# Gated cross attention with routed experts: value stores, attention's first loads and the last y store under other waits

## The reference

```python
def _L0_xattn_ref(x, cross_input, ...):
    q, k, v = _heads(x @ Wq + bq), _heads(x @ Wk + bk), _heads(x @ Wv + bv)
    att = jnp.einsum('bhqd,bhkd->bhqk', q, k) * scale
    att = jnp.where(causal[None, None], att, -jnp.inf)
    y = jnp.einsum('bhqk,bhkd->bhqd', jax.nn.softmax(att, axis=-1), v)
    ...
    y = y + jnp.einsum('bhqk,bhkd->bhqd', jax.nn.softmax(attc, axis=-1), vc)
    return y @ Wp + bp

x = x + jnp.tanh(g_xattn[0]) * _L0_xattn_ref(_layernorm(x, axis=-1), ctx_512, ...)
x = x + jnp.tanh(g_ffn[0]) * _L0_ffn_ref(_layernorm(x, axis=-1), ...)
```

## Time and profile before

| | us |
|---|---|
| median of 3 runs | 2671.09 |
| lowest and highest | 2663.04, 2671.52 |
| the profiled execution | 2655.1 |
| its span | 2653.1 |

### The profile page before, as it was taken

One profiled execution on the slowest core, in us unless ns is written; L12 is line 12 of the kernel. 1 busy time (PEld: TensorE's weight loads), 2 busy tenths in 40 slices (PEclk: granted clock), 3 DMA queues, 4 the chain that ended last, 5 costly groups with the idle time before them and its releaser, 6 DMA issues. The chain is left out here.

```text
span 2653.1 us, 55050 instructions
## 1 busy us (share of the span) xinstructions
PE 2456.7 (93%) x20198; PEld 1487.9 (56%) x20198; DVE 1927.3 (73%) x3194; ACT 1574.4 (59%) x3344; POOL 462.5 (17%) x534
## 2 busy tenths in 40 slices
PE   6886999999999999999999999988999999998897
PEld 6775444444444444444444444477788877787785
DVE  8766888888888888888888888566533644544557
ACT  4441577777777777777777777843244433442442
POOL 2001100101010101010010101022332423422514
PEclk9897899999999999999999999987999999999998
DMA  7999674756566564747465654242134322422533
GB/s 255 395 363 289 90 106 77 96 84 85 91 79 89 80 96 65 104 65 95 81 89 87 82 86 69 55 154 98 57 121 127 116 70 78 120 68 68 170 102 104
DMA packets 163778, 305.66 MB, mean 115 GB/s; under 512 B 44455, under 2 KB 111150, under 8 KB 155182
## 3 DMA queue, kind: packets, MB, share of 16 engines
q1 hardware_dynamic: 150174, 265.53, 48.1%
q0 software_dynamic: 12288, 33.57, 4.0%
q10 hardware_dynamic: 1072, 3.23, 0.5%
HBM read 165.10 MB, written 127.68 MB: 110 GB/s over the span
## 5 line engine op out<-in xcount | busy, mean ns | idle before, releaser
L811 ACT ACTIVATE at_P<-at_ST 128x512 f32<-128x512 f32 (+4 forms) x2176 | 1095.9, 559 | 372.5 <-PE at_ST L854 350.3
L762 DVE TENSOR_REDUCE f_part<-at_R 128x2 f32<-128x804 f32 x1024 | 976.0, 994 | 121.4 <-PE at_R L842 117.0
L869 PE MATMUL at_OP<-at_P,at_V 128*32 128x256 f32 x8192 | 642.0, 385 | 16.0 <-ACT at_O L819 12.9
L854 PE MATMUL at_ST<-at_Q,at_K 64*128 64x512 f32 (+4 forms) x1428 | 343.7, 455 | 3.5 <-ACT at_P L811 3.5
L869 PEld LDWEIGHTS at_OP<-at_P,at_V 128*32 128x32 f32 x8192 | 163.3, 108 | 264.2 <-ACT at_P L811 185.7
L842 PE MATMUL at_R<-at_K,at_Q 64*128 64x402 f32 x1344 | 271.2, 392 | 5.1 <-DVE f_part L762 5.1
L745 POOL TENSOR_SCALAR_AFFINE_SELECT at_P<-at_P 128x512 f32<-128x512 f32 x128 | 81.6, 637 | 1089.1 <-ACT at_P L811 1089.1
L854 PEld LDWEIGHTS at_ST<-at_Q,at_K 64*128 64x128 f32 (+1 forms) x1428 | 141.6, 180 | 218.5 <-ACT at_P L811 203.6
L759 DVE TENSOR_REDUCE f_mx<-at_R 128x2 f32<-128x256 f32 (+3 forms) x256 | 209.9, 821 | 42.8 <-PE at_R L835 40.7
L1825 DVE TENSOR_TENSOR ex_ab<-ex_bank,ex_sg 128x256 f32<-128x256 f32 x148 | 62.8, 424 | 226.1 <-ACT ex_sg L1908 167.4
L842 PEld LDWEIGHTS at_R<-at_K,at_Q 64*128 64x128 f32 x1344 | 128.0, 185 | 115.8 <-issue 69.2
(11 more groups left out here) (246 smaller groups left out, 4170.3 us busy)
## 6 DMA issues: line engine op xcount, KB each, us to landing
at_K<-k_parts SPq DMA_DIRECT2D x126, 264.1 KB, 9.2
k_parts<-pj_kpart SPq DMA_DIRECT2D x32, 800.5 KB, 8.5
expert_rows<-ex_rb SPq DMA_DIRECT2D x148, 128.0 KB
ex_xb<-sorted SPq DMA_DIRECT2D x72, 256.0 KB
v_items<-pj_vbuf SPq DMA_DIRECT2D x32, 544.0 KB, 8.0
q_parts<-pj_qpart SPq DMA_DIRECT2D x32, 512.0 KB, 10.6
at_Q<-q_parts SPq DMA_DIRECT2D x252, 64.0 KB, 9.6
f_K<-k_parts SPq DMA_DIRECT2D x60, 264.1 KB, 9.9
```

Source lines behind the costliest of these rows:

```text
L762: dve.tensor_reduce(part[:, :, p, q, c], buf[:, :, 0:XC], AX.X, ALU.max).then_inc(s_drain, 1)
L811: act.activation(Pt[(NKT * n + s) % NP][0:rows, h, c0:T], ST[(NST * n + s * G + h) % NB][0:rows, c0:T], ACT.Exp, scale=SCALE).then_inc(s_e ...
L854: pe.matmul(ST[t % NB][0:rows, c0:T], K[n % NU][half, p, keys], Q[n % NU][half, kind, p, c0:T], start=True, stop=True).then_inc(s_st, 1)
L869: ins = pe.matmul(OP[32 * h:32 * h + 2 * D, at], V[n % 2][0:rows, key_tile(s), h, :], Pt[(NKT * n + s) % NP][0:rows, h, at], start=s in (0 ...
```

## The change

The four value stores of a batch become one that covers the same rows; the value tag's semaphore counts 16 a batch instead of 64. SP's `load(1)` waits for batch 0's stores only, and ahead of the first load of each later batch's items SP waits for that batch's stores. GpSimd fills `K1`'s ones first, and waits for the stores and fills `V`'s ones behind it; the thresholds of `s_one` follow this order. The last y store counts up a semaphore of its own, `s_ylast`; SP no longer waits for it at the end of attention, but in `load_y` of the last batch.

```diff
 def written(tag, batches):
-    return (64 if tag == "v" else 32) * batches + 1
+    return (16 if tag == "v" else 32) * batches + 1
...
-                    for g in range(NG):
-                        dst = VS.rearrange("(b g) p t c -> b g p t c", b=B)[bass.ds(b, 1), g]
-                        sp.dma_start(dst.rearrange("o p t c -> (o p) t c"), vbuf[:, g]).then_inc(s_wr["v"], 16)
+                    dst = VS.rearrange("(b g) p t c -> b p g (t c)", b=B)[bass.ds(b, 1)]
+                    sp.dma_start(dst.rearrange("o p g c -> (o p) g c"), vbuf[:, :, :, :].rearrange("p g t c -> p g (t c)")
+                                 ).then_inc(s_wr["v"], 16)
...
-                            dve.wait_ge(s_wr["v"], 64 * b + 1)
+                            dve.wait_ge(s_wr["v"], 16 * b + 1)
...
                         if r == 2 and n < NU:
-                            sp.wait_ge(s_one, 2 * n + 2)
+                            sp.wait_ge(s_one, 4 * (n - 1) + 2)
...
-                    sp.dma_start(YS[n // NG, :, :, n % NG * GC:(n % NG + 1) * GC], ysum[n % 2][:, :, :]).then_inc(s_yst[n % 2], 16)
-
-                for n in WRITES:
-                    sp.wait_ge(first.s_wr[n], written(n, B))
+                    sp.dma_start(YS[n // NG, :, :, n % NG * GC:(n % NG + 1) * GC], ysum[n % 2][:, :, :]).then_inc(
+                        s_yst[n % 2] if n < NI - 1 else early.s_ylast, 16)
+
+                def batch_written(b):
+                    for n in WRITES:
+                        sp.wait_ge(first.s_wr[n], written(n, b + 1))
+
+                batch_written(0)
                 load(1)
...
                     if n + 2 < NI:
+                        if (n + 2) % NG == 0:
+                            batch_written((n + 2) // NG)
                         load(n + 2)
...
                 for u in range(2):
-                    sp.wait_ge(s_yst[u], 16 * (NI // 2))
+                    sp.wait_ge(s_yst[u], 16 * ((NI - u) // 2))
...
                     if b >= 2:
                         sp.wait_ge(s_T, b - 1)
+                    if b == B - 1:
+                        sp.wait_ge(early.s_ylast, 16)
                     sp.dma_start(y[b % 2][:, :, :], YS[b]).then_inc(s_y[b % 2], 16)
```

More of the change, by code:

```diff
@@ L712, in _ @@
             def _(pool):
[L713 to L716, removed]
                 def ones(n):
                     for h in range(2):
-                        pool.wait_ge(s_one, 2 * n + h)
+                        if n > 1 or h:
+                            pool.wait_ge(s_one, 4 * (n - 1) + h)
                         pool.memset(K[n][64 * h + 32:64 * h + 64, :, :].bitcast(F32), 1.0).then_inc(s_one, 1)
-                    pool.wait_ge(s_one, 2 * n + 2)
+                    pool.wait_ge(s_one, 4 * (n - 1) + 2)
                 def values(n):
@@ L734, in _ @@
                 ones(1)
+                for n in WRITES:
+                    pool.wait_ge(first.s_wr[n], written(n, B))
+                for u in range(2):
+                    pool.memset(V[u][:, :, :, D:2 * D], 1.0).then_inc(s_one, 1)
                 values(0)
@@ L916, in __init__ @@
         self.s_y, self.s_w, self.s_b, self.s_r = (r_.sem(n) for n in ("y0", "w", "b", "r"))
+        self.s_ylast = r_.sem("ylast")
         self.s_f = [r_.sem(f"f{u}") for u in range(2)]
```

## The result

| | before | after |
|---|---|---|
| median | 2666.78 us (16 runs) | 2660.16 us (16 runs) |
| lowest and highest | 2660.92, 2674.18 | 2651.1, 2666.29 |
| the profiled execution's span | 2653.1 us | 2664.3 us |

The ratio is 0.9975, with a 95% interval of 0.9964 to 0.9986: 6.7 us less, between 3.7 and 9.6. The forecast was a ratio of 0.9981, 5.1 us. The interval holds it.

What follows compares the result with a forecast made beforehand. Transfers were taken to bound projection, and TensorE, ScalarE and VectorE together to pace attention. Terms 3.4 + 0 + 0 + 1.7 = 5.1 us gave ratio 0.9981, 2666.0 us from a median of 2671.09; range 2656 to 2676.

Steps and rivals of the forecast that it cites:

- The rounds: Projection's 8 rounds: one value store lands when four did, so VectorE's wait in 7 rounds stays; 0 us.
- C: Rival, projection rounds: the single store lands earlier, VectorE's wait shrinks 1.5 us each, 10.5 us more off; 2655.4, chance 0.12.
- D: Rival, projection rounds: the single store drains slower, VectorE's wait grows, 1.8 us a round; 2678.6, chance 0.10.
- The estimate beside C: Projection rounds: by the skill's fixed part, four stores 13.1 us, one 7.1; 6 us a round, 42 in all.
- The first border: Projection to attention: all engines wait for SP's four issues, 3.97 us; a single one takes 0.59, saving 3.4 us.
- B: Rival, first border: SP must stay for the whole single store, so only 1.7 us come off; 2669.4, chance 0.17.
- The loads: Start of attention: loads waiting for their own batch and ones filled at once move up, but nobody waits; 0 us.
- The second border: Attention to mixing: SP no longer awaits the last y store's landing; 1.7 us off on all engines.
- TensorE's clock (E): Rival, both borders: shorter gaps keep TensorE's clock high, 2.4 us more off; 2663.6, chance 0.17.
- The sum: Whole kernel: 3.4 us at the first border, 1.7 at the second, 0 elsewhere; 5.1 us, ratio 0.9981.

Runs made afterwards that it cites:

- e9: The kernel before with one value store per batch plus a second of the same bytes to a spare tensor, awaited too: 2641.60 us, ratio 1.0162.
- e6: The kernel before with one value store in batches 0 to 6 and four in the last: 2597.96 us, ratio 1.0002.
- e1: The kernel before with only the value stores made one per batch; loads, ones and last y store as before: 2596.42 us, ratio 0.9994.
- e5: The kernel before with one value store in the last batch alone, four in batches 0 to 6: 2596.85 us, ratio 0.9989.
- e3: The kernel before with only the loads waiting for their own batch and K1's ones filled first; four value stores: 2598.14 us, ratio 1.0001.
- e12: The changed kernel, but GpSimd waits for the stores and fills V's ones before K1's, as before: 2593.21 us, ratio 0.9977 against before.
- e4: The whole change on the second experiment chip, against the kernel before: 2591.31 us, ratio 0.9973.
- e2: The kernel before with only the last y store on its own semaphore, awaited by batch 7's load: 2595.86 us, ratio 0.9987.
- e11: The kernel before with one value store per batch and item 0's context shift rows issued by ScalarE on its queue: 2603.75 us, ratio 1.0024.

## Why the prediction was right, point by point

**The rounds, 0: right.** VectorE waits 43.9 us instead of 45.9, and between 41.4 and 46.2 in all traces but e9's. That bytes and not transfers set the rounds is shown by e6 and e9 together. C and D fall. The estimate beside C, 42 us by the Trainium skill's fixed part, rested on a fit for transfers that GpSimd issues, and nothing of it is seen.

**The first border, 3.4 us: right in place and nearly in size.** The issue takes 0.38 us and not the 0.59 taken from the y rows; from it to the first matmul 4.42 us became 0.83: 3.6. That SP might have to stay (B) falls. The nearest row was x's 0.38 with as many rows, not the y rows' 0.59.

**The loads, worth 0: this step failed.** The prediction said that "the load is 6 us early today" and that "what is moved up also costs nothing", and of the border that "all of it stands 3.4 us earlier". It looked for the readers of `K1` and found them late. It named item 0's shift rows, 16 KB in all, only as the next thing on SP's queue, and left out that they lie behind the load in the same line and that TensorE's first scores need them. load(1) starts at the landing of the stores, and the border's edit does not move that, while it moves the scores 3.6 us up. Without the loads' part TensorE waits 3.8 us (e1) or 2.5 us (e5), and the gain of 3.6 is gone or mostly gone. So the part is worth 0 alone (e3, ratio 1.0001) and, by the waits, up to 3.8 us behind the border's edit. The first half of the part, waiting for the own batch, brings this; of the early ones no effect is seen (e12). The sum came out right because the change holds both; that was luck, for nothing in the prediction says that the two parts need each other.

**The second border, 1.7 us: right in place, 1.5 in size.** With the landing no longer awaited, the first matmul comes 0.7 us after SP's issue ends, not the 0.5 us that it came after the landing.

**TensorE's clock (E): half seen, worth nothing.** Behind the gap of 1.8 us the clock stays high at first, but falls within the phase of maxima, as the argument against E said: the windows of after have 0.65 from 240 to 244 and 0.50 from 244 on, and it is still 0.50 at the first scores. The first exponential comes 38.08 us behind the first matmul in after and 38.33 in before, so 0.25 us at most came of it. At the second border the eight transposes take 1.94 us as before, behind a gap of 2.9.

**The sum.** The traces give 3.6 + 1.5 = 5.1 us, the forecast's own sum. The measured 6.7 us, and 7.0 by the ratio in e4 (7.7 by the medians), lie above it, and 5.1 lies within both intervals (3.7 to 9.6, 4.4 to 9.4). The nearest to a surplus is e2, 3.4 us where its trace shows 1.5, again within its interval. Whether 2 us more come off somewhere is open: of the stretches looked at, the rounds, the rest of attention and what follows show nothing beyond their spread of 4 to 5 us, which is wider than that.

## What to carry to other kernels

Before an issue or a wait is cut from a border, list what starts by another clock, here loads that wait for a landing, and what small transfer lies behind them in the line: the stage moves up, they do not, and the smallest copy may become the last. Price parts of a change in the company in which they will run, since two edits can be worth next to nothing alone and 3.4 us together. Where SP leads a border, count the issues that stand between its last input and the meeting; of the four 544 KB stores here the first took 0.33 us and the later ones up to 1.18.

## What the runs showed that was not expected

- One transfer of 2.23 MB in 512 rows takes SP 0.38 us to issue, four of a quarter each 3.9 to 4.0 and two 1.6. The size of a store does not show in its issue here; that it goes out right behind another one does.
- Four copies of 4 KB came in 7.5 us (e1, SP's queue, behind load(1)) and 11 us (e11, ScalarE's, beside load(2)) after the last of them was issued, while loads of long rows to few partitions kept the DMA engines at a share of 0.91 to 1.11 with only 106 to 124 GB/s (e1, windows from 252 to 276 us): the engines were full by time, not by bytes.
